# Expert stage of a two-layer model on one core: each transpose between two gate and up products instead of behind them

## The reference, cut to what matters

```python
E, K, H, F = (64, 6, 512, 192)
CAP = 2 * (T * K // E)        # T = 512: 96 rows for an expert
x = x + tanh(g_xattn[0]) * L0_xattn_ref(layernorm(x), ...)   # four experts, one for each token
x = x + tanh(g_ffn[0])   * L0_ffn_ref(layernorm(x), ...)     # dense, block-quantised
x = x + tanh(g_xattn[1]) * L1_xattn_ref(layernorm(x), ...)
x = x + tanh(g_ffn[1])   * L1_ffn_ref(layernorm(x), ...)     # the expert stage:

buf = zeros((E, CAP + 1, H)).at[se, slot].set(x[tok])[:, :CAP]
h = silu(einsum('ech,ehf->ecf', buf, w_gate)) * einsum('ech,ehf->ecf', buf, w_up)
out = einsum('ecf,efh->ech', h, w_down)
gathered = out[se, pos] * valid[:, None]
y = segment_sum(gathered * w, tok, num_segments=Tn)
```

## Time and profile before

| what | value |
|---|---|
| median of 3 runs | 1038.74 us (1033.59 to 1039.02) |
| span of the profiled execution, first to last instruction | 1035.2 us |
| PE busy in it | 963.8 us, 93% |
| expert stage, from its first gate and up product to its last down product | about 698 to 998.5 us of the span |
| one pass of the pair loop | 9.35 us |
| granted TensorE clock in the stage | 1.00 of full speed |

### The profile page before, as it was taken

One profiled execution on the slowest core, in us unless ns is written; L12 is line 12 of the kernel. 1 busy time (PEld: TensorE's weight loads), 2 busy tenths in 40 slices (PEclk: granted clock), 3 DMA queues, 4 the chain that ended last, 5 costly groups with the idle time before them and its releaser, 6 DMA issues.

```text
span 1035.2 us, 13635 instructions
## 1 busy us (share of the span) xinstructions
PE 963.8 (93%) x4408; PEld 474.7 (46%) x4430; DVE 622.8 (60%) x1168; ACT 418.9 (40%) x817; POOL 633.9 (61%) x569
## 2 busy tenths in 40 slices
PE   6998999859999999899999999999999999999992
PEld 4454555424444444344444445335555555555530
DVE  5796978258888887777777778962222222222221
ACT  5565656224444443666666654331111111111100
POOL 4687887358888897886667651344554455444430
PEclk9999999989999999999999999999999999999996
DMA  8556351360000001500002405178999999999848
GB/s 274 157 189 213 115 160 62 66 127 1 1 1 1 2 1 41 203 22 22 21 21 80 185 1 204 60 262 283 342 339 334 337 332 332 336 337 338 242 64 184
DMA packets 64788, 162.90 MB, mean 157 GB/s; under 512 B 9760, under 2 KB 9904, under 8 KB 64336
## 3 DMA queue, kind: packets, MB, share of 16 engines
q1 hardware_dynamic: 47360, 116.94, 32.5%
q0 software_dynamic: 17360, 45.10, 18.3%
HBM read 129.67 MB, written 35.48 MB: 160 GB/s over the span
## 4 chain that ended last, share of the span: by engine, by line
PE 56%; POOL 8%; DVE 8%; issue 5%; ACT 2%; DMA 1%; DVEq 0%; POOLq 0%; ACTq 0%
PE PS L1607 16%; PE PS L1626 9%; PE PS L1442 6%; PE PS L1454 6%; PE PS L1431 6%; POOL ARENA L672 4%; PE PS L1596 3%; PE PS L369 3%; PE PS L1396 2%; POOL ARENA L678 2%; PE PS L1415 2%; DVE ARENA L1227 1%; DVE CT L1226 1%; PE PS L1615 1%; DMA X<-gain 1%
## 5 line engine op out<-in xcount | busy, mean ns | idle before, releaser
L727 POOL TENSOR_TENSOR ARENA<-ARENA 128x512 f32<-128x512 f32 x128 | 133.2, 1062 | 52.8 <-DVE ARENA L1038 52.8
L773 POOL DMA_INDIRECT out<-ARENA,idx x32 | 45.8, 1431 | 124.6 <-DVE ARENA L1259 107.9
L1396 PE MATMUL PS<-SLAB,ARENA 128*128 128x512 bf16 x501 | 116.2, 382 | 3.3 <-ACT ARENA L1748 2.1
L1880 ACT ACTIVATE ARENA<-PS 96x192 f32<-96x192 f32 x64 | 20.9, 326 | 226.8 <-PE PS L1607 226.8
L1259 DVE COPY ARENA<-PS 96x512 f32<-96x512 f32 x64 | 41.1, 682 | 94.0 <-PE PS L1626 94.0
L1787 ACT ACTIVATE ARENA<-PS,ARENA 128x512 f32<-128x512 f32 x128 | 86.8, 683 | 18.1 <-DVE ARENA L1032 14.9
L1607 PE MATMUL PS<-SLAB,ARENA 128*96 128x384 f32 x240 | 81.1, 490 | 0.1
L1032 DVE TENSOR_REDUCE ARENA<-PS 128x2 f32<-128x1024 f32 x64 | 78.1, 1221 | 5.0 <-PE PS L1431 4.9
L1442 PEld LDWEIGHTS PS<-ident,ARENA 128*128 128x128 f32 x512 | 54.8, 141 | 52.0 <-issue 36.6
L1396 PEld LDWEIGHTS PS<-SLAB,ARENA 128*128 128x128 bf16 x512 | 49.5, 98 | 60.6 <-issue 4.5
L678 POOL TENSOR_TENSOR ARENA<-ARENA 128x1024 bf16<-128x1024 fp8e4 x32 | 61.1, 1908 | 23.2 <-DVE ARENA L999 23.1
(11 more groups left out here) (268 smaller groups left out, 1851.9 us busy)
## 6 DMA issues: line engine op xcount, KB each, us to landing
SLAB<-in_L_ffn_w_gate SPq DMA_DIRECT2D x30, 384.0 KB, 20.7
SLAB<-in_L_ffn_w_up SPq DMA_DIRECT2D x30, 384.0 KB, 20.8
X<-in_L_ffn_w_down SPq DMA_DIRECT2D x14, 768.0 KB, 21.9
SLAB<-in_L_ffn_w_down SPq DMA_DIRECT2D x10, 768.0 KB, 21.9
CT<-in_L_ffn_w_gate SPq DMA_DIRECT2D x16, 384.0 KB, 21.0
CT<-in_L_ffn_w_up SPq DMA_DIRECT2D x16, 384.0 KB, 20.7
X<-in_ctx SPq DMA_DIRECT2D x4, 1024.0 KB, 8.7
XNT<-in_L_ffn_w_gate SPq DMA_DIRECT2D x16, 256.0 KB, 2.6
```

What stands on the lines that cost most here:

```text
L727: last = pool.tensor_tensor(prob[s % 4][:, h, :], prob[s % 4][:, h, :], rec[:, s % 4, h:h + 1].to_broadcast([P, D]), ALU.mult)
L1396: last = pe.matmul(bank(b), QT[:, par, k * P:(k + 1) * P], w[:, k, c * D:(c + 1) * D], start=(k == 0), stop=(k == KD - 1))
```

## The change

`turn_rows` and `turn_h6` are cut into their single transposes. `gate_up6(e, turned, hidden_of)` issues, behind each of its four products, one transpose of the rows of expert `turned`, and behind the first three also one of the hidden values of pair `hidden_of`. In the pair loop gate_up6(2t + 2) carries the rows of expert 2t + 4, gate_up6(2t + 3) those of expert 2t + 5 and the hidden values of pair t. The waits that stood ahead of a run of transposes now stand ahead of its first one, so in the middle of a gate_up6. ACT's order follows: silu6(e), bt(e + 2), silu6(e + 1), bt(e + 3). Nothing is added or taken away. The programs of DVE, POOL and SP are the same as before.

```diff
-                def turn_rows(e):
-                    pe.wait_ge(g_in6[e % GR], 16 * (e // GR) + 16)
-                    need(pe, bt_out, e - 1)
-                    for k in range(KD):
-                        last = pe.transpose(bank(e % 2)[:, k * CAP:(k + 1) * CAP], xg[0:CAP, e % GR, k:D:KD], ident[0:CAP, 0:CAP])
-                    last.then_inc(row_turned, 1)
-
-                def gate_up6(e):
+                def turn_rows(e, k):
+                    if k == 0:
+                        pe.wait_ge(g_in6[e % GR], 16 * (e // GR) + 16)
+                        need(pe, bt_out, e - 1)
+                    last = pe.transpose(bank(e % 2)[:, k * CAP:(k + 1) * CAP], xg[0:CAP, e % GR, k:D:KD], ident[0:CAP, 0:CAP])
+                    if k == KD - 1:
+                        last.then_inc(row_turned, 1)
+
+                def turn_h6(t, m):
+                    if m == 0:
+                        pe.wait_ge(h6_ready, 2 * t + 2)
+                        need(pe, ht6_out, t - 1)
+                    last = pe.transpose(bank(6 + t % 2)[:, m * CAP:(m + 1) * CAP], h6[0:CAP, t % 2, :, m:F1:3], ident[0:CAP, 0:CAP])
+                    if m == 2:
+                        last.then_inc(h6_turned, 1)
+
+                def gate_up6(e, turned=None, hidden_of=None):
...
-                    last.then_inc(gu6_done, 1)
...
+                        if k == KD - 1:
+                            last.then_inc(gu6_done, 1)
+                        if hidden_of is not None and k < 3:
+                            turn_h6(hidden_of, k)
+                        if turned is not None:
+                            turn_rows(turned, k)
...
                     if t + 1 < PAIRS:
-                        gate_up6(2 * t + 2)
-                        gate_up6(2 * t + 3)
-                    turn_h6(t)
-                    if t + 2 < PAIRS:
-                        turn_rows(2 * t + 4)
-                        turn_rows(2 * t + 5)
+                        gate_up6(2 * t + 2, 2 * t + 4 if t + 2 < PAIRS else None)
+                        gate_up6(2 * t + 3, 2 * t + 5 if t + 2 < PAIRS else None, t)
+                    else:
+                        for m in range(3):
+                            turn_h6(t, m)
                     down6(t)
...
-                for t in range(PAIRS):
-                    if t + 1 < PAIRS:
-                        silu6(2 * t + 2)
-                        silu6(2 * t + 3)
-                    if t + 2 < PAIRS:
-                        bt(2 * t + 4)
-                        bt(2 * t + 5)
+                for e in range(E1):
+                    silu6(e)
+                    if e + 2 < E1:
+                        bt(e + 2)
```

More of the change, by code:

```diff
@@ L1632, in _ @@
                     pe.matmul(bank(0), ident[:, :], XG[:, GCH - 1, 0, :], start=True, stop=True)
[L1633 to L1638, removed]
+                for e in range(2):
+                    for k in range(KD):
+                        turn_rows(e, k)
+                for e in range(2):
+                    gate_up6(e)
+                    for k in range(KD):
+                        turn_rows(e + 2, k)
                 for t in range(PAIRS):
                     if t + 1 < PAIRS:
-                        gate_up6(2 * t + 2)
-                        gate_up6(2 * t + 3)
-                    turn_h6(t)
-                    if t + 2 < PAIRS:
-                        turn_rows(2 * t + 4)
-                        turn_rows(2 * t + 5)
+                        gate_up6(2 * t + 2, 2 * t + 4 if t + 2 < PAIRS else None)
[3 more added lines that the diff above has]
+                            turn_h6(t, m)
                     down6(t)
```

## The result

The changed kernel takes 1048.91 us (median, 1047.64 to 1051.17) against 1037.97 us. The ratio of the runs is 1.0131, with a 95% interval of 1.0102 to 1.0161. The same two kernels, timed once more against each other, gave 1.0121 (1.0094 to 1.0148). The medians differ by 10.9 us, the ratio makes 13.6. The forecast was +14 us (1053, range 1042 to 1062).

The account below looks back on a forecast made before the run. PE alone bounded the kernel, with gathered rows arriving just in time. Slower passes gave +15.5 us, the stage's end -0.65, fewer add waits -1: +14 on 1038.7, so 1053 us, range 1042 to 1062.

Parts of the forecast that it names:

- The margin: Expert stage before the change: gathered rows land typically 3.75 us (even) and 1.25 us (odd) before use, zero in the worst pass.
- The loop: Down products, copy, add, gather, 7.8 us landing, transpose, rest of pass: spans two passes and sets a pass of 9.92 us.
- the loop of the even rows: Two passes through the even experts' gather, landing and transposes: 19.64 us, so 9.82 us a pass.
- the scatter: Landing times vary by a good half microsecond around the median and each pass awaits the later: 0.1 us added per pass.
- the odd loop: Two passes through the odd experts' gather, landing and transposes: 19.51 us, so 9.75 us a pass.
- The way from the odd landing to the end of the pass: PE's remaining work in a pass from the odd rows' transpose on: 9.16 - 3.78 = 5.38 us.
- What PE's profile was to show: Expert stage: 1 to 2 us idle before row transposes in most passes, busy share about 0.92, clock unchanged.
- PE alone: PE's own work per pair-loop pass, without waits: 9.16 us instead of 9.35, with lone transposes at 0.09 us.
- The first pass of the loop: First pass using a gather issued in the pair loop: 2.3 us of waiting, 1.8 us more than the others' 0.57.
- The last passes and the end: After the last weights land, about three passes run at 9.16 us; at t = 30 a product covers a 0.55 us wait.
- The sum: All terms of the expert stage together: +14.9 us, less 1 us for adds waiting less often, giving +14.
- The one that would have made the change faster: Gathers land in time, under about 6.5 us, leaving only PE's gain of 5.8 and 0.65 us: some 1032 us, chance 0.06.

## Why the prediction was right, and where it was off

*The margin.* Right, and the step that carried all. That the gathered rows landed just before use in the kernel before made the place of their waits decisive. The run with the waits moved alone shows it without any other part of the change. One thing was not told apart: the margin was worked out with one landing time, 7.8 us, for both kinds of gather, but those of odd experts, whose margin was the smaller, land later (7.9 us against 7.7, medians over all).

*The loop.* Right in its form: the chain of the changed kernel runs through landing, transposes, down products, copy, add and gather. Its size was 9.92 us a pass. The passes t = 3 to 25 begin at 733.98 and end at 961.74, 9.90 us each:

```profile
733.98 0.89 PE L1617 MATMUL PS<-XNT,ARENA 128*96 128x384 f32 x2
...
961.74 0.89 PE L1617 MATMUL PS<-CT,ARENA 128*96 128x384 f32 x2
```

The sum got there by terms that were off against each other. It took 9.82 us from the loop of the even rows and added 0.1 for the scatter. In most links of the measured chain it is the odd gather, and with its median of 7.9 us the odd loop is longer than the 9.75 of the prediction. The way from the odd landing to the end of the pass was also taken too short, 5.38 us, since a transpose that has waited takes longer to start the products behind it: the odd landing of the chain shown above ends at 768.15, and the next pass begins 5.5 us later. 6.33 + 7.9 + 5.5 us are 9.87 us a pass. The landings of even experts were shorter than taken (7.5 instead of 7.8). That the changed kernel's view of the landings says 7.2 us is no sign of faster landings, since it holds 13 of 53 gathers:

```profile
DMA to landing us min/median/max: 3.7/7.2/8.4
```

*What PE's profile was to show.* Two signs were off. PE's busy share in the stage was to fall to about 0.92 and is 229.28 / 240 = 0.96, and waits of 1 to 2 us in most passes were expected, but in 700 to 1010 there are 19, of 0.64 us in the mean. A wait costs more than its idle time: the passes t = 3 to 25 take 17.8 us more than at 9.13 each, and the idle time for rows in them is some 10 us. The third, an unchanged clock, did not hold at t = 2.

*PE alone.* I took 9.16 us a pass; it is 9.13, read where nothing waits, in the run with two gathers ahead. A lone transpose costs just under 0.09 us, as chosen, the second of two 0.11 to 0.12.

*The first pass of the loop.* This term was mis-sized. I gave it 1.8 us above the others, as a wait of 2.3. The wait was 1.99 us, but the pass took 733.98 - 720.95 = 13.04 us, 3.7 more than before:

```profile
720.95 0.89 PE L1617 MATMUL PS<-X,ARENA 128*96 128x384 f32 x2
723.82 0.43 PE L1596 MATMUL PS<-ident,ARENA 96*128 96x96 f32 x1 [1.99 <-DMA ARENA<-rows,idx]
724.05 1.49 PE L1617 MATMUL PS<-X,ARENA 128*96 128x384 f32 x2
```

```profile
723.00:727.00 4.00, 3.18 (x8) 1.65 (x9) 0.00 (x0) 0.00 (x0) 3.39 (x3) 0.61 1.05 329
```

The products behind the wait ran at half the clock: 1.49 us for two records instead of 0.81, a mean granted clock of 0.61 in those 4 us. The repeat had a wait of 1.83 us there, kept its clock and took 11.24 us for the pass, so the clock made about 1.7 of the 13.04 us. The prediction had no term for it.

*The last passes and the end.* Right in kind. The gathers started after 970 land in 3.7 us, and four passes instead of three, t = 26 to 29, are back at PE's own pace; the last of them takes 998.25 - 989.12 = 9.13 us. At t = 30 no wait is left in front of the down products, where the earlier trace rows had 0.55 us:

```profile
989.12 0.89 PE L1617 MATMUL PS<-SLAB,ARENA 128*96 128x384 f32 x2
...
998.25 3.47 PE L1617 MATMUL PS<-X,ARENA 128*96 128x384 f32 x10
...
1003.10 0.81 PE L1617 MATMUL PS<-X,ARENA 128*96 128x384 f32 x2
1003.84 2.82 PE L1634 MATMUL PS<-X,ARENA 64*96 64x512 f32 x12
```

*The sum.* The forecast was +14 us; the ratio makes +13.6, the repeat +12.5, and the plain medians +10.9 both times. That it came so close is partly luck. In the first pair of traces the stage is 15.1 us longer, 315.1 against 300.0. The pass t = 2 cost 1.3 us more than forecast because of the clock, and 23 passes instead of 25 were slow, which gave 1.6 us back. In the second pair the stage is only 9.5 us longer, 312.3 against 302.8: there the clock did not fall, and the kernel before had waits of its own, for which the forecast had no term.

*The rivals.* The one that would have made the change faster needed landings under 6.5 us. With lighter weights the median over all gathers fell to 6.1 and the time went back to that of the kernel before, in the region where the prediction had put the turn. Named for that rival was the Trainium skill, page DMA: Bandwidth & Descriptors, section on the anatomy of one DMA, with its fit of 2.0 us plus the bytes at 436 GB/s. The trace comes near to it only when no weights are queued, 3.7 us against the 2.5 us estimated from it.

## What to carry to other kernels

Before moving work to an earlier place, read when its input arrives, not only whether its engine waits for it today; an engine that never waits may have a margin of zero. A wait in the middle of a run of products holds all that is behind it, and where the results of that run set off the next transfers, it closes a loop whose length is set by the transfer's landing. If the input can be asked for earlier at no cost, as here by two gathers into slots that were free already, do that first, and the same move that lost 1.3% gains 0.8% together with it (about a fifth of that is from the earlier requests alone).

## What the runs showed of the hardware that was not expected

After a wait of 1.99 us in a PE that was otherwise busy, the granted clock went from the 2.4 GHz level to the 1.2 GHz level for a few microseconds; after a wait of 1.83 us at the same place in the repeat, and after one of 2.2 us in the pass t = 8 of the run with the waits moved, it did not. What decides it is left open.

The landing time of a 96-row gather was 3.7 us with no weights queued, 6.1 to 6.2 us (medians over all gathers started in 725 to 950) with the DMA engines at a share of 0.90, and 7.3 to 7.9 us at 1.03 to 1.05. The same kernel showed medians of 7.8 and 7.9 us and maxima of 9.0 and 9.4 us in two executions, and that was enough for it to wait in one and hardly in the other.
